# Both halves of the weighing of the values in one turn of TensorE's loop

## The reference, cut to what matters

```
scores = einsum('bhqd,bhkd->bhqk', q, k) / sqrt(8)
scores = where(mask, scores, -inf)          # first: causal; third: by a prefix sum of boundaries; second and fourth: none
probs  = softmax(scores, axis=-1)
ctx    = einsum('bhqk,bhkd->bhqd', probs, v)
out    = ctx.reshape(B, S, 128) @ wo + bo
```

## Time and profile before

| | |
|---|---|
| median of three runs | 1808.96 us (1808.39 to 1814.23) |
| the profiled execution's own time | 1808.39 us |
| its span in the trace | 1806.4 us |
| TensorE matmuls busy | 1404.4 us, 78% of the span |
| VectorE busy | 1239.0 us, 69% |
| ScalarE busy | 916.9 us, 51% |
| mean granted clock of TensorE | 0.879 of full speed |

### The profile page before, as it was taken

One profiled execution on the slowest core, in us unless ns is written; L12 is line 12 of the kernel. 1 busy time (PEld: TensorE's weight loads), 2 busy tenths in 40 slices (PEclk: granted clock), 3 DMA queues, 4 the chain that ended last, 5 costly groups with the idle time before them and its releaser, 6 DMA issues. The chain is left out here.

```text
span 1806.4 us, 31936 instructions
## 1 busy us (share of the span) xinstructions
PE 1404.4 (78%) x10666; PEld 854.3 (47%) x10666; DVE 1239.0 (69%) x4823; ACT 916.9 (51%) x2002; POOL 339.1 (19%) x360
## 2 busy tenths in 40 slices
PE   5998978972874769995455799999992995778984
PEld 2454434441763534442234456666662884444542
DVE  7888377975336868897766677677665224658987
ACT  4664366651322346655622577777761442137766
POOL 3320022111534125400021000000002333302200
PEclk9999999985997879996577799999995997679996
DMA  3220014211561023310010000000003573002300
GB/s 128 55 54 2 0 19 59 37 36 47 161 142 33 12 53 54 54 19 20 1 60 1 13 7 7 13 7 7 1 1 106 163 200 96 26 19 43 56 10 24
DMA packets 59361, 83.42 MB, mean 46 GB/s; under 512 B 8064, under 2 KB 46208, under 8 KB 58688
## 3 DMA queue, kind: packets, MB, share of 16 engines
q1 hardware_dynamic: 54208, 71.15, 15.7%
q0 software_dynamic: 4992, 10.23, 2.9%
HBM read 51.18 MB, written 9.18 MB: 33 GB/s over the span
## 5 line engine op out<-in xcount | busy, mean ns | idle before, releaser
L876 ACT ACTIVATE L_xattn_probs<-ps 128x1024 f32<-128x1024 f32 x192 | 196.7, 1025 | 106.6 <-PE ps L1069 105.1
L717 DVE TENSOR_REDUCE maxs<-ps 128x4 f32<-128x1024 f32 x128 | 156.5, 1223 | 20.0 <-PE ps L1045 18.6
L3503 ACT ACTIVATE wide_pr<-wide_sc,wide_nm 128x256 f32<-128x256 f32 x256 | 127.0, 497 | 13.2 <-DVE wide_nm L3431 12.7
L1085 PE MATMUL ps<-L_xattn_probs,values 128*32 128x256 f32 x1536 | 122.5, 392 | 1.7 <-ACT L_xattn_qs L948 1.7
L1579 POOL DMA_INDIRECT moe_xs<-normed,moe_table x92 | 87.4, 950 | 156.6 <-PE ps L1609 73.4
L3426 DVE COPY wide_prT<-ps 128x512 f32<-128x512 f32 x64 | 44.3, 692 | 84.5 <-PE ps L3544 84.4
L711 DVE CUSTOM_DVE_ANT_0 L_xattn_masked_scores<-ps,L_xattn_maskQ 128x256 bf16<-128x256 f32 x256 | 93.1, 420 | 9.9 <-PE ps L1045 8.9
L1045 PE MATMUL ps<-keys,L_xattn_qs 64*128 64x256 bf16 x768 | 75.7, 275 | 26.3 <-DVE maxs L717 11.4
L3401 DVE CUSTOM_DVE_ANT_0 wide_sc<-ps,wide_mask 128x256 f32<-128x256 f32 x256 | 93.2, 419 | 3.3 <-PE ps L3529 2.3
L2008 DVE SCALAR_TENSOR_TENSOR moe_z_sb<-ps,moe_wt,moe_a_sb 128x256 f32<-128x256 f32 x46 | 22.2, 484 | 93.6 <-ACT moe_a_sb L2039 93.6
L1069 PE MATMUL ps<-L_xattn_qm,keys 64*128 64x256 bf16 x768 | 74.6, 272 | 5.6 <-ACT L_xattn_probs L876 4.1
(11 more groups left out here) (629 smaller groups left out, 3632.2 us busy)
## 6 DMA issues: line engine op xcount, KB each, us to landing
moe_wt<-in_packed_experts SPq DMA_DIRECT2D x23, 707.0 KB
moe_wt<-in_packed_experts SPq DMA_DIRECT2D x23, 384.0 KB
keys<-L_xattn_k_parts SPq DMA_DIRECT2D x108, 64.0 KB
L_xattn_qs<-L_xattn_q_parts SPq DMA_DIRECT2D x108, 64.0 KB
expert_out<-moe_y SPq DMA_DIRECT2D x46, 128.0 KB
weights<-in_packed_L_xattn SPq DMA_DIRECT2D x2, 1316.0 KB, 7.3
keys<-L_attn_k_parts SPq DMA_DIRECT2D x36, 64.0 KB
L_attn_qs<-L_attn_q_parts SPq DMA_DIRECT2D x36, 64.0 KB
```

Of the source, the lines that this page charges most:

```text
L717: v.tensor_reduce(nm, ps[:, BANK_M:BANK_M + 2, :].rearrange("p j (t n) -> p j t n", t=2), AX.X, ALU.max, negate=True).then_inc(S("m_used"), 1)
L876: a.activation(probs[:, s % RING, :, :, :].rearrange("p j t n -> p j (t n)"), ps[:, BANK_P:BANK_P + 2, :], ACT.Exp, scale=HD ** -0.5)\
L1085: mm = pe.matmul(ps[32 * j:32 * j + 32, BANK_V, q0:SEQ], V[:, m % 2 * PT + 2 * b + kt, (g % GROUPS) * 4 + j, :], probs[:, (2 * g + j // 2) ...
L3503: ins = a.activation(pr[:, s % 3, j, qt, :], sc[:, s % 2, j, qt, :], ACT.Exp, bias=nm[:, s % 2, n:n + 1], accum_out=sums[:, s % 2, n:n + 1])
```

## The change

`weigh_values` of a group is no longer split over an even and an odd turn. Both calls are issued in turn 2g+5, where the second was before, still ahead of `max_scores`. In even turns nothing stands between `turn_max` and `max_scores`. The one wait for `q_ready`, which keeps the first group from writing a bank that still holds a query, moves along and asks for 5 where it asked for 6. Number, shape and data of all matmuls stay the same, and no other engine's program is touched. All four attention sublayers are affected, with 32 groups each.

```
                         turn_max(s - 1)
-                    g, kt = divmod(s - 4, 2)
-                    if 0 <= g < SLOTS // 2:
-                        if s == 4:
-                            pe.wait_ge(S("q_ready"), 6)
-                        weigh_values(g, kt)
+                    g, odd = divmod(s - 5, 2)
+                    if not odd and 0 <= g < SLOTS // 2:
+                        if g == 0:
+                            pe.wait_ge(S("q_ready"), 5)
+                        weigh_values(g, 0)
+                        weigh_values(g, 1)
                     if 0 <= s + 1 < SLOTS:
                         max_scores(s + 1)
```

## The result

The changed kernel takes 1825.9 us (median of 8, 1818.1 to 1833.4), the kernel before 1809.5 on the same chip (8, 1808.2 to 1814.2). The ratio is 1.0084, interval 1.0066 to 1.0101: about 15 us slower. The forecast had the direction, but the size was double the +7 that I had summed, and the time lies above the range. The profiled execution took 1817.4 (span 1815.4), less than the median; experiments 1 and 2 say what that is worth.

The account below looks back on a forecast made before the run. Each attention turn was taken to cost the larger of VectorE's loop and TensorE's queue. Unmasked +5.4, third attention +1.8, first -0.3 and ends +0.4 gave +7.3 us on 1808.39, 1815.7, stated as 1816 for the median; range 1807 to 1823.

Parts of the forecast that it names:

- The floor that VectorE sets: Attention turns: L1045 waits until L717 has read the single score banks, so at least 1.72 us unmasked, 1.96 third attention.
- Rival A: All attention turns: TensorE's queue sets most, each pair of calls saves 0.14 us, 18 us in all, 1791; chance 0.10.
- The price of the second call: Odd turns: the second call adds 0.43 us, so a full pair costs 1.00, or 0.79 in the causal sublayer.
- B's earlier overlap: Odd turns: the queue overlaps more than counted, 0.05 us less in some 110 turns, 1810, no change; chance 0.20.
- C's dearer call: Odd turns: second call costs 0.57 us, 0.14 more in some 110 turns, 1831; 0.05 dearer gives 1821; chance 0.12.
- it would stay at 1404: Sign for the profile after: TensorE's busy time stays at 1404 us within a few us.
- what costs nothing: Other engines: ScalarE's copy, GpSimd, DMA queues and the moved q_ready wait were given no cost in the sum.
- ends of the four: End of each attention: the last but one group ends behind the last slot's exponentials, about +0.1 us each, +0.4.
- the gain of 0.57 in turns of the rotation: First attention, where rotation projections fill even and odd turns: even turns gain 0.57 us in full against 0.43 lost.
- the mark for slower: Whole time: slower begins at 1814.4 us, as a measurement tells about 0.3%, or 5.4 us, from no change.

Follow-up runs that it names:

- experiment 1: The changed kernel run again with no edit, for a second profile: 1831.4 us, ratio 1.0069 to the kernel before.
- experiment 2: The kernel before run again with no edit, for a second profile: 1813.7 us.
- experiment 12: The changed kernel with ScalarE's copy L960 made by VectorE at the end of its odd turn: 1825.9 us, ratio 1.0093 to the kernel before.
- experiment 6: The changed kernel with both calls of a group in even turn 2g+4 instead of odd turn 2g+5: 1836.1 us, ratio 1.0123 to the kernel before.
- experiment 7: The changed kernel with four more weighing matmuls, read by nothing, in each even turn: 1842.5 us, ratio 1.0165 to the kernel before.
- experiment 4: The change in the two unmasked attentions alone (second and fourth), old order elsewhere: 1826.0 us, ratio 1.0043 to the kernel before.
- experiment 5: The changed kernel with ScalarE's copy L960 moved behind its side work in the odd turn: 1823.2 us, ratio 1.0045 to the kernel before.

## Why the forecast had the direction and not the size

**The floor that VectorE sets: right.** It is 1.72, 1.96 and 1.64 in the three kinds of sublayer, under every kernel but that of experiment 12, which puts more work on VectorE. No turn fell below it. Experiments 6 and 7 show that neither fewer nor more calls move it. Rival A (1791) is refuted by this: TensorE's busy time did fall, by 15 us where the saved breaks promised 18, and the time rose. (Its reading of the earlier trace rows was wrong, though: PE is busy over 90% in three of the stretches, not two.)

**The price of the second call: right.** It is 1.00 for a pair in all turns where L1045 follows at once, and 0.79 in most turns of the causal sublayer. B's earlier overlap and C's dearer call are both out. What the step did not see is that busy PE falls with it; I had said that it would stay at 1404.

**The step that failed: the floor of a shortened even turn was taken from VectorE alone, and ScalarE was put at nothing.** The prediction has "ScalarE's copy (L960) waited for the second call before and waits for it now, at the same place in the turn" under what costs nothing. The place is the same (0.13 behind L1045 in both), but the turn is shorter, and ScalarE's own chain (1.92 and 0.15 to L1069) was hidden by 0.02 us only. By window, predicted and measured:

| | predicted | measured |
|---|---|---|
| unmasked, second attention, without turns 15 to 17 | 0, +0.9, +1.0, +0.8 | +1.2, +1.5, +1.5, +0.9 |
| unmasked, fourth attention (experiment 4) | +0.2, +0.8, +1.0, +0.8 | +1.5, +1.6, +1.5, +0.9 |
| third attention | 0, +0.5, +0.7, +0.6 | +0.8, +0.8, +0.9, +0.8 |
| first attention | -0.3 in all | +0.1, +0.8, +0.5, +0.1 |
| ends of the four | +0.4 | +0.5 |

Over undisturbed turns the change costs 15.0 us where I had 6.9 (the 7.3 less 0.4 for the ends). Of the 8 us between, experiment 5 gives 5.1 back by moving the copy, which is shown: 0.3, 1.0, 0.5 and 0.1 in the four windows of each unmasked attention, 0.8 in the third attention and 0.4 in the first. With the copy last, the first windows outside the first attention are still 2.1 us above my sum and the first attention 1.4, while the second windows lie 0.9 below it. In first windows it is the loop of 2.84 us: I had counted a gain for the even turn there (6.47 to 6.37 for turns 4 and 5, which became 6.90). The loop is read in the rows. Experiments 5 and 12 agree, since moving the copy left those turns as they were, and so does experiment 7, where added work in turn 4 left the pair at 6.90. No run shortened the loop itself. In the first attention the gain of 0.57 in turns of the rotation is the term that did not come in full (turns 6 and 7 went from 5.80 to 6.06, where I had a small gain). What holds these turns back was not tested.

One step of the chances was off as well: I said that a third of my own forecast lies below the mark for slower, and then multiplied by 0.8. That changes no time.

**The turns at the border, partly open.** At the border of the first and second window L1045 needs the queries that twelve transfers lay out (L487). In the second attention it waits for them in every profile, before and after, and there 2.7 us of the loss disappear: turns 15 to 17 took 5.98 + 3.35 + 2.15 before and 4.73 + 1.72 + 2.32 after. A part of this is chance, since the 3.35 had a granted clock of 0.50 from 288 to 290, and experiment 1 has 4.67 + 2.20 + 3.18. So it is luck that this stretch grew by 2.4, close to the 2.7 that I had for it. In the fourth attention the wait came and went: turn 15 took 1.81 before, 2.74 in the same kernel again, 4.02 after, 2.59 in experiment 1 and 2.07 in experiment 12. The rows of after there:

```profile
1662.43 1.07 PE L1085 MATMUL ps<-L_xattn_probs,values 128*32 128x256 f32 x16
...
1665.36 0.39 PE L1045 MATMUL ps<-keys,L_xattn_qs 64*128 64x256 bf16 x4 [1.86 <-issue]
1665.79 1.23 DVE L717 TENSOR_REDUCE maxs<-ps 128x4 f32<-128x1024 f32 x1 [2.46 <-PE ps L1045]
```

and the views of stretches, after and then before (the last number is GB/s, the one before it the share of the DMA engines):

```profile
1651.00:1656.00 5.00, 4.79 (x64) 2.44 (x64) 3.94 (x12) 3.64 (x7) 0.52 (x1) 1.00 0.57 71
1656.00:1660.00 4.00, 2.99 (x42) 1.46 (x38) 3.71 (x8) 3.58 (x7) 1.88 (x3) 1.00 0.57 78
...
1664.00:1672.00 8.00, 6.43 (x58) 3.90 (x58) 4.86 (x10) 3.11 (x5) 0.00 (x0) 0.79 0.16 33
```

```profile
1651.00:1656.00 5.00, 4.68 (x58) 2.29 (x58) 4.29 (x12) 4.08 (x8) 0.55 (x1) 1.00 0.56 99
1656.00:1660.00 4.00, 3.53 (x42) 1.60 (x41) 3.76 (x9) 3.80 (x7) 2.37 (x3) 1.00 0.38 94
...
1664.00:1672.00 8.00, 7.84 (x92) 4.30 (x93) 7.50 (x19) 5.59 (x9) 1.09 (x1) 1.00 0.36 54
```

In these windows the DMA engines moved 71 to 78 GB/s where they had moved 94 to 99. The wait and the slow clock behind it are 3.3 of the 8.8 us by which this stretch grew: this turn is 4.02 where experiment 12, without a wait, has 2.07, and turn 17 is 3.72 where experiment 1 has 2.32.

The long wait comes with the low rate in every profile. Over the 8 us from the first of these twelve issues the rate is 72 to 75 GB/s in the second attention of all fourteen profiles, and turn 15 takes 4.35 to 6.13 there. In the fourth attention it is 85 to 100 in the five profiles of kernels that leave this attention's calls as they were (turn 15: 1.81 to 2.74). In the nine others it is 72 to 75 in five (3.48 to 4.47), 80 in one (2.59) and 95 to 100 in three (1.87 to 2.10). So the wait is not the change's alone. Whether the change makes the low rate likelier can't be told from so few profiles, and why the rate differs stays open.

The undisturbed turns alone (15.0) are as much as the 15 us that were measured, and the ends add 0.5. The border turns gave 2.7 and took 3.7 in the profile after (1.4 and 0.9 in experiment 1).

## What to carry to other kernels

A turn of a hand-ordered loop has a floor for each engine that takes part, not one. Before counting a gain in a shorter turn, follow every chain that ends in it back to the turn's start, ScalarE's too, and note how little hides it (here 0.02 us). Work moved from one turn to the next is a loss wherever the giving turn stands at such a floor and the taking turn has no slack for it, even if the move saves busy time on the fullest engine.

## What the runs showed of the hardware that I had not expected

- Two adjacent calls of four column strips cost 0.57 and 0.43 us up to the next L1045, not only at the end of an attention but everywhere in the loop. TensorE's busy time falls with it: 15.4 us for 128 pairs.
- While the same twelve transfers of 64 KB ran, the DMA engines moved 72 to 75 or 85 to 100 GB/s (once 80), in two stretches of one execution and in executions of nearly the same program.
- After TensorE had waited 1.9 us in the fourth attention, the mean granted clock was 0.79 of full speed from 1664 to 1672 (row above; 1.00 before the change). From 1668 to 1670 it was 0.50, the lower of the two levels (1.2 and 2.4 GHz). An x16 that takes 1.07 elsewhere took 1.46 in it. Such a stretch cost 1.4 us here (turn 17: 3.72 against 2.32) and 1.3 us in turn 2 of the third attention (3.80 at a granted clock of 0.55, 2.50 at 1.00). The same kernel had it in one profile and not in the other.
